# A message-passing layer on one core: clears held to four in flight, first stage in a new order, two results kept in PSUM

## The reference, cut to what matters

```
ssp(v) = softplus(v) - log 2
h   = x @ W_in2f
W   = (ssp(edge_attr_64 @ Wf1 + bf1) @ Wf2 + bf2) * edge_weight1
m   = segment_sum(h[dst] * W, src, 50000)
m   = ssp(m @ Wo1 + bo1) @ Wo2 + bo2
out = layernorm(x + (x + m))
```

## Time and profile before

| | us |
|---|---|
| median of 3 runs | 1865.61 (1861.05 to 1866.87) |
| profiled execution | 1858.28, its span 1856.5 |
| busy in the span: PE | 1697.3 |
| DVE | 1489.3 |
| ACT | 1492.9 |
| POOL | 1441.4 |
| first stage: last scatter ends | 1398.4 |
| second stage: first PE work | 1403.57 |

### The profile page before, as it was taken

The page is one execution under the profiler, slowest core; times in us unless marked ns, Lnnn a source line. Parts: engine busy times, 40 slices in busy tenths (PEclk is TensorE's granted clock), DMA queues, the critical chain, the costliest instruction groups (busy, mean ns, idle before and its releaser), DMA issues. The chain is left out here.

```text
span 1856.5 us, 36676 instructions
## 1 busy us (share of the span) xinstructions
PE 1697.3 (91%) x11376; PEld 1532.2 (83%) x11376; DVE 1489.3 (80%) x3750; ACT 1492.9 (80%) x2945; POOL 1441.4 (78%) x1385
## 2 busy tenths in 40 slices
PE   3499899999999999999999998889976999999995
PEld 2378788888888888888888887778866999999995
DVE  2477788787888888888888786777765999999996
ACT  2477788778888788888888786776756999999996
POOL 7422488888887888878888888888754999999997
PEclk9699999999999999999999998999998999999998
DMA  9799866656566665666665666665675999999994
GB/s 354 251 356 372 266 123 112 126 112 125 115 125 122 112 123 114 124 125 112 125 120 116 119 122 113 114 118 108 116 185 170 333 363 362 360 360 364 357 366 174
DMA packets 177341, 363.47 MB, mean 196 GB/s; under 512 B 25622, under 2 KB 76264, under 8 KB 177148
## 3 DMA queue, kind: packets, MB, share of 16 engines
q1 hardware_dynamic: 101128, 257.75, 39.8%
q0 software_dynamic: 75136, 102.45, 32.4%
q10 hardware_dynamic: 884, 0.92, 0.2%
HBM read 206.90 MB, written 154.12 MB: 194 GB/s over the span
## 5 line engine op out<-in xcount | busy, mean ns | idle before, releaser
L354 POOL DMA_INDIRECT acc<-sums,src_ix x392 | 637.2, 1626 | 141.6 <-issue 116.0
L341 POOL DMA_INDIRECT xg<-in_x,dst_t x392 | 401.4, 1024 | 215.6 <-issue 114.6
L780 DVE SCALAR_TENSOR_TENSOR m_l<-pair,wgt_t,m_h 128x256 fp32r<-128x256 f32 x392 | 171.6, 479 | 230.5 <-ACT m_h L621 206.6
L385 POOL TENSOR_SCALAR sums<-sums,neg_mean,rstd 128x256 f32<-128x256 f32 x392 | 283.2, 733 | 10.2
L495 PE MATMUL pair<-m_h,same 128*128 128x256 f32 (+1 forms) x980 | 244.8, 285 | 30.4 <-ACT sums L628 21.9
L621 ACT ACTIVATE m_h<-pair,wgt_t 128x256 fp32r<-128x256 f32 x392 | 165.0, 475 | 99.5 <-PE pair L409 57.6
L495 PE MATMUL pair<-m_l,same 128*128 128x256 f32 (+1 forms) x980 | 241.8, 281 | 0.0
L409 PE MATMUL pair<-wo_h,msg_h 128*128 128x256 f32 (+1 forms) x784 | 230.9, 295 | 6.0 <-DVE m_l L780 5.2
L495 PEld LDWEIGHTS pair<-m_h,same 128*128 128x128 f32 (+1 forms) x980 | 185.1, 189 | 52.2 <-issue 34.9
L576 ACT ACTIVATE zs<-pair,bf 128x512 f32<-128x512 f32 x196 | 124.1, 685 | 125.8 <-PE pair L433 99.5
L409 PE MATMUL pair<-wo_h,msg_l 128*128 128x256 f32 (+1 forms) x784 | 222.0, 283 | 0.0
(11 more groups left out here) (97 smaller groups left out, 5249.8 us busy)
## 6 DMA issues: line engine op xcount, KB each, us to landing
acc<-fill SPq DMA_DIRECT2D x197, 256.0 KB
xg<-in_x SPq DMA_DIRECT2D x97, 512.0 KB, 6.4
sums<-acc SPq DMA_DIRECT2D x97, 512.0 KB, 6.8
out<-sums SPq DMA_DIRECT2D x97, 512.0 KB, 4.7
attr<-in_edge_attr SPq DMA_DIRECT2D x196, 128.0 KB
srcb<-in_src_rows SPq DMA_DIRECT2D x98, 256.0 KB
xg<-in_x,dst_t POOLq DMA_INDIRECT x392
acc<-sums,src_ix POOLq DMA_INDIRECT x392
```

What stands on the lines that cost most here:

```text
L341: pool.indirect_dma_start(xg[0:g.p, g.xs, r], None, t["x"], bass.IndirectOffsetOnAxis(ap=dst_t[0:g.p, r, g.n:g.n + 1], axis=0)).then_inc(x ...
L354: pool.indirect_dma_start(acc, bass.IndirectOffsetOnAxis(ap=src_ix[g.slot][0:g.p, r:r + 1], axis=0), sums[0:g.p, g.slot, r], None, compute ...
L385: last = pool.tensor_scalar(normed[0:g.p, g.n % NRING, r], res[0:g.p, u, r], neg_mean[0:g.p, u, r:r + 1], rstd[0:g.p, u, r:r + 1], ALU.add ...
L780: dve.scalar_tensor_tensor(out=m_l[0:g.p, r], in0=bank[6][0:g.p, k * D:(k + 1) * D], scalar=col(wgt_t, r, g), in1=m_h[0:g.p, r].bitcast(F3 ...
```

## The change

- SP: every clear waits for the clear four before it (four semaphores); the wait for the first gather after 8 clears is gone; the last rows are part of the same loop, so there are 198 clears in it.
- Rings: `RING` 12 to 13, `XRING` 11 to 12, `AHEAD` 23 to 24.
- The softplus result is written over its PSUM banks 2 and 3, and the message over bank 5, in place of the SBUF tiles `ssp` and `msg`, which are gone. `ssp_high`, `ssp_low`, `msg_high`, `msg_low` read PSUM. So `filter1` now waits for `ssp_low`, and `w_of` for `msg_low`.
- The three orders are new. `summed(0)` has lag 2 (was 3) and stands last, `summed(1)` keeps lag 3; `keep_y` has lag 3 (was 4); `compare` is four stages; most ACT and DVE stages have a lag less.
- SP: x for the second stage is loaded a group a step in the last steps, not at once at the end.
- `biases` is a piece of `first_weights` that now comes before step 0. Tiles of the second stage lie elsewhere.

```diff
-RING = 12
-XRING = 11
+RING = 13
+XRING = 12
-AHEAD = 23
-EARLY_CLEARS = 8
+AHEAD = 24
+IN_FLIGHT = 4
...
             def clear_to(count):
                 nonlocal clears
                 for c in range(clears, min(count, CLEARS)):
-                    sp.dma_start(acc[c * CLEAR * P:(c + 1) * CLEAR * P, :].rearrange("(p k) d -> p (k d)", k=CLEAR), fill[:, 0:CLEAR].rearrange("p k d -> p (k d)")).then_inc(cleared, 16)
+                    a, b = c * CLEAR * P, min((c + 1) * CLEAR * P, N + R * P)
+                    wait(sp, cleared[c % IN_FLIGHT], c // IN_FLIGHT * 16)
+                    sp.dma_start(acc[a:b, :].rearrange("(p k) d -> p (k d)", k=CLEAR),
+                                 fill[0:(b - a) // CLEAR].rearrange("p k d -> p (k d)")).then_inc(cleared[c % IN_FLIGHT], 16)
                 clears = max(clears, min(count, CLEARS))
-            clear_to(EARLY_CLEARS)
-            sp.wait_ge(xg_in[0], 16 * R)
             clear_to(FIRST_CLEARS)
...
                 clear_to(FIRST_CLEARS + (n - 1) * CLEARS_A_STEP)
+                if G - XRING <= n - 2:
+                    fetch_x(group((n - 2) % XRING))
...
-                wait(pe, ssp_sb, g.n * H)
+                wait(pe, sspl_sb, g.n * H)
...
-                    wait(pe, msg_sb, g.n * H + m)
+                    wait(pe, msgl_sb, g.n * H + m)
...
-            run((w_of(1), 2), (summed(0), 3), (h_of(0), 1), (summed(1), 3), (filter1, 0), (turn_x(0), 0),
-                (out1(0), 2), (turn_x(1), 0), (w_of(0), 1), (h_of(1), 1), (out1(1), 2), before={1: filter_bias})
+            run((w_of(1), 2), (summed(1), 3), (turn_x(0), 0), (turn_x(1), 0), (out1(0), 2), (h_of(0), 1), (filter1, 0),
+                (w_of(0), 1), (out1(1), 2), (h_of(1), 1), (summed(0), 2), before={1: filter_bias})
...
-            run((keep_y(0), 4), (msg_high(1), 3), (ssp_high(0), 2), (ssp_high(1), 2), (keep_h(0), 2), (absolute(0), 1),
-                (absolute(1), 1), (expo(0), 1), (m_high(0), 3), (keep_y(1), 4), (expo(1), 1), (x_high(0), 1), (loga(0), 1),
-                (loga(1), 1), (x_high(1), 1), (keep_h(1), 2), (m_high(1), 3), (a_high, 0), (msg_high(0), 2), before={1: weights})
+            run((x_high(0), 1), (keep_y(0), 3), (x_high(1), 1), (ssp_high(0), 1), (msg_high(1), 2), (ssp_high(1), 1), (keep_y(1), 3),
+                (a_high, 0), (m_high(0), 2), (keep_h(0), 1), (absolute(0), 0), (absolute(1), 0), (expo(0), 0), (expo(1), 0),
+                (loga(0), 0), (loga(1), 0), (msg_high(0), 1), (m_high(1), 2), (keep_h(1), 1), before={1: weights})
...
-                    dve.scalar_tensor_tensor(out=msg[:, m], in0=bank[5][:], scalar=bias_w[:, m:m + 1], in1=h_sb[:, m],
+                    dve.scalar_tensor_tensor(out=bank[5][:], in0=bank[5][:], scalar=bias_w[:, m:m + 1], in1=h_sb[:, m],
...
-                    low(msg_l[:, m], msg[:, m].rearrange("f (r e) -> f r e", r=R), msg_h[:, m], msgl_sb)
+                    low(msg_l[:, m], bank[5][:].rearrange("f (r e) -> f r e", r=R), msg_h[:, m], msgl_sb)
...
-                    dve.scalar_tensor_tensor(out=ssp[:, h], in0=bank[2 + h][:], scalar=neg_bf1[:, h:h + 1], in1=zs[:, h],
+                    dve.scalar_tensor_tensor(out=bank[2 + h][:], in0=bank[2 + h][:], scalar=neg_bf1[:, h:h + 1], in1=zs[:, h],
...
-                    low(ssp_l[:, g.par, h], ssp[:, h].rearrange("m (r e) -> m r e", r=R), ssp_h[:, g.par, h], sspl_sb)
+                    low(ssp_l[:, g.par, h], bank[2 + h][:].rearrange("m (r e) -> m r e", r=R), ssp_h[:, g.par, h], sspl_sb)
...
-            run((m_low(0), 3), (message(0), 2), (x_low(0), 1), (softplus(0), 1), (softplus(1), 1), (x_low(1), 1),
-                (m_low(1), 3), (message(1), 2), (a_low, 0), (msg_low(0), 2), (target, 3), (msg_low(1), 2), (ssp_low(0), 1),
-                (ssp_low(1), 1), (compare, 2), before={1: first_weights, 2: tables, 3: second_weights})
+            run((x_low(0), 1), (message(1), 2), (x_low(1), 1), (msg_low(1), 2), (ssp_low(0), 1), (ssp_low(1), 1), (a_low, 0),
+                (compare(0), 2), (m_low(0), 2), (compare(1), 2), (compare(2), 2), (message(0), 1), (compare(3), 2), (softplus(0), 0),
+                (msg_low(0), 1), (softplus(1), 0), (m_low(1), 2), (target, 2),
+                before={0: biases, 1: first_weights, 2: tables, 3: second_weights})
```

More of the change, by code:

```diff
@@ L155, in build @@
         a_h, a_l = (sb(n, [P, R, P], F32R) for n in ("a_h", "a_l"))
-        zs, ssp = (sb(n, [P, H, 512]) for n in ("zs", "ssp"))
+        zs, h_sb = (sb(n, [P, H, 512]) for n in ("zs", "h_sb"))
         ssp_h, ssp_l = (sb(n, [P, 2, H, R, P], F32R) for n in ("ssp_h", "ssp_l"))
@@ L173, in build @@
         grown = [zs, h_sb]
-        ssp2, ssp2_h, ssp2_l = [ssp, msg], ssp_h, ssp_l
+        ssp2 = [sums[:, MRING + DEPTH + NRING + k].rearrange("p r d -> p (r d)").rearrange("p (h n) -> p h n", h=H) for k in range(2)]
+        ssp2_h, ssp2_l = ([b[:, k] for k in range(2)] for b in (ssp_h, ssp_l))
         wo2 = attr[:, G % ARING].rearrange("p (h d) -> p h d", h=H)
@@ L181, in build @@
         dst_in, src_in, wgt_in, tab_made = sem("dst_in"), sem("src_in"), sem("wgt_in"), sem("tab_made")
-        bo1_in, fill_made, cleared = sem("bo1_in"), sem("fill_made"), sem("cleared")
+        bo1_in, fill_made = sem("bo1_in"), sem("fill_made")
+        cleared = [sem(f"cleared{u}") for u in range(IN_FLIGHT)]
         made = sem("made")
@@ L224, in build @@
         block = ctx.enter_context(nc.Block())
-        CLEARS = N // P // CLEAR
+        CLEARS = -(-(N + R * P) // (P * CLEAR))
         TABLES = 1 + R
-        assert N // P % CLEAR == 0
-        CLEAR_REST = len(range(CLEARS * CLEAR * P, N + R * P, CLEAR * P))
+        assert (N + R * P) % CLEAR == 0
         def rows_of(ap, g):
@@ L293, in fetch_m @@
                 sp.dma_start(m_in[0:g.p, g.n % MRING].rearrange("p r d -> p (r d)"), rows_of(acc, g).rearrange("(p r) d -> p (r d)", r=R)).then_inc(m_got[g.n % MRING], 16)
[L295 to L299, removed]
             def store(g):
@@ L304, in store @@
                 sp.dma_start(rows_of(out, g).rearrange("(p r) d -> p (r d)", r=R), normed[0:g.p, u].rearrange("p r d -> p (r d)")).then_inc(stored[u], 16)
-            for n in range(G - XRING, G):
+            for n in range(G - 1, G):
                 fetch_x(group(n % XRING))
@@ L348, in stage @@
                         if g.n == 0:
-                            pool.wait_ge(cleared, 16 * (CLEARS + CLEAR_REST))
+                            for u in range(IN_FLIGHT):
+                                pool.wait_ge(cleared[u], 16 * len(range(u, CLEARS, IN_FLIGHT)))
                         pool.wait_ge(src_ready, g.n + 1)
@@ L526, in stage @@
                             for sp2, w in ((ssp2_h, wo2_h), (ssp2_h, wo2_l), (ssp2_l, wo2_h)):
-                                last = pe.matmul(o, sp2[:, g.par, h, r, 0:g.p], w[:, h, :], start=False, stop=h == H - 1 and sp2 is ssp2_l)
+                                last = pe.matmul(o, sp2[g.par][:, h, r, 0:g.p], w[:, h, :], start=False, stop=h == H - 1 and sp2 is ssp2_l)
                     last.then_inc(o_ps, 1)
@@ L736, in a_low, with compare, stage @@
                 low(a_l[:, :, 0:g.p], attr[:, g.n % ARING].rearrange("f (r e) -> f r e", r=R)[:, :, 0:g.p], a_h[:, :, 0:g.p], al_sb)
-            def compare(g):
-                dve.wait_ge(srcb_in[g.n % SRING], (g.n // SRING + 1) * 16)
-                wait(dve, y_ps, (g.n - 1) * 2)
-                sources = srcb[0:g.p, g.n % SRING].rearrange("x (r e) -> x r e", r=R)[:, :, 0:g.p]
-                for a in range(R):
+            def compare(a):
+                def stage(g):
+                    if a == 0:
+                        dve.wait_ge(srcb_in[g.n % SRING], (g.n // SRING + 1) * 16)
+                        wait(dve, y_ps, (g.n - 1) * 2)
+                    sources = srcb[0:g.p, g.n % SRING].rearrange("x (r e) -> x r e", r=R)[:, :, 0:g.p]
                     dve.scalar_tensor_tensor(out=same[0:g.p, g.par, FROM[a]:FROM[a] + R - a, 0:g.p], in0=sources[:, a:R],
@@ L746, in compare @@
                                              accum_out=alike[0:g.p, g.par, a:a + 1]).then_inc(same_ready, 1)
+                return stage
             def target(g):
@@ L818, in ssp2_low @@
                 wait(dve, o_ps, (g.n - 1) * 2)
-                low(ssp2_l[:, g.par].rearrange("m h r e -> m (h r e)"), ssp2[g.par][:].rearrange("m h n -> m (h n)"),
-                    ssp2_h[:, g.par].rearrange("m h r e -> m (h r e)"), ssp2l_sb)
+                low(ssp2_l[g.par].rearrange("m h r e -> m (h r e)"), ssp2[g.par][:].rearrange("m h n -> m (h n)"),
+                    ssp2_h[g.par].rearrange("m h r e -> m (h r e)"), ssp2l_sb)
             def residual(g):
```

24 lines of the change are left out of this document (12 added, 12 removed).

## The result

The changed kernel takes 1891.03 us (median of 4 runs, 1888.32 to 1892.29) against 1865.21 for the kernel before in the same comparison: ratio 1.014, 95% interval 1.0119 to 1.0161. Slower by 26 us, where 18 us faster was forecast; the range of 1820 to 1879 does not hold it. The profiled execution has a span of 1886.6 us against 1856.5: 30.1 us to explain.

What follows compares the result with a forecast made beforehand. It took POOL and PE to finish the first stage nearly together, after a head paced by SP's clears. Terms -17 + 0 - 7 + 6 gave -18 us: execution 1840, median 1848, range 1820 to 1879.

Steps and rivals of the forecast that it cites:

- The head: The stretch up to about 212 us: `filter1` of group 12 was to start at 202 against 218.8, 17 us earlier.
- A clear costs 0.97, 1.10 and 0.80 us with four in flight: Head, SP's clears: 0.97 us for the first 36, 1.10 for the next 16, 0.80 late.
- The third rival: Head: the hold starves the clears, 1.0 us each from the start, 30 us on the head, +12, 1878; chance 0.10.
- The hold cures the early stalls: Head: ACT's 13.3 us and DVE's 37.6 us stalls, read as instruction fetch queued behind clears, were to go.
- SP's list of clears sets the first scatter: Head: SP's list sets the pace and reaches group 12's load at 194, with the first scatter at 199.
- PE's step: Groups 12 to 97: 13.36 us a step against 13.35 before, so 0 over 85 steps.
- the ring: Longest dependency chain from one `filter1` to the next in the new order, through DVE and ACT: 13.06 us.
- The stalls took 0.33: ACT stalls that PE feels: 0.36 us a step in the old order, 0.30 forecast in the new.
- the 0 that was taken for them: DVE passes writing PSUM: no extra time per pass, within -0.05 to +0.15 us; two passes lie in the ring.
- POOL's cover: Scatters and gathers less disturbed by DVE: up to 30 us less on POOL, mostly cover, not time.
- The drain: From `filter1` of group 97 to the last scatter's end: 38 us against 45, 7 us less.
- the 6: Near the end: 6 us given back, as POOL, nearly tied with PE, delays x.

Runs made afterwards that it cites:

- e2: The kernel before with only the hold added (four clears in flight): 1888.52 us, ratio 1.014.
- e1: The changed kernel without the hold on clears: 1879.63 us, ratio 1.0071 against the kernel before.
- e6: The kernel before with no clears in the first step, then 20 a step: 1895.66 us in a single run.
- e5: The kernel before with POOL's first gathers paced by the groups turned, clears untouched: 1863.1 us, ratio 0.999.
- e4: The changed kernel with the old rings (`RING`, `XRING`, `AHEAD` 12, 11, 23): 1887.75 us, ratio 1.0117 against the kernel before.
- e16: The changed kernel, its own order, without the hold and with paced gathers: 1834.63 us, ratio 0.987 against the kernel before.
- e17: The changed kernel without the hold and with paced gathers, run again on another chip: 1870.07 us, ratio 1.0015 against the kernel before.
- e9: The kernel before with 68 clears first in place of 36: 1886.88 us, ratio 1.0134.
- e10: The changed kernel without the hold, with 84 clears first in place of 36: 1860.41 us, ratio 0.9999 against the kernel before.
- e3: The changed kernel with softplus and message back in SBUF tiles and the old rings: 1936.33 us, ratio 1.0375 against the kernel before.
- e7: The changed kernel with three other orders, whose longest ring is PE's own 12.6 us, hold kept: 1916.5 us, ratio 1.0276 against the kernel before.
- e8: The changed kernel with three other orders, without the hold and with paced gathers: 1883.08 us, ratio 1.0093 against the kernel before.
- e11: The kernel before with paced gathers and 24 clears a step in place of 16: 1897.28 us, ratio 1.0192.

## Why the prediction was wrong

**The head, -17, was +22.5, and this step alone turns the sign.** Three of its claims failed.
- *A clear costs 0.97, 1.10 and 0.80 us with four in flight.* It costs 1.22, 1.40 and 0.80 to 0.92. The value was chosen near an idle load of 196 KB; the other bound, 1.18 from the 512 KB stores under load, was the better guide, since these clears run beside gathers and loads too. e2 prices the hold at 23.5 us in the old order, e1 at 11 in the new one. The third rival had this mechanism, with 1.0 us a clear from the start, 30 us on the head and a time of 1878; its size was too small, and it got 0.10.
- *The hold cures the early stalls, since these are engines whose instruction fetch is queued behind clears.* The stalls grew from 37.6 to 54.9 us on DVE and from 13.3 to 35.7 on ACT. e6 took the early clears away and kept the stall; e5 paced the gathers and cut it to 11.9. `filter1` of group 2 tells which part of the change lengthens the stall: it starts at 77.2 us before and at 78.8 with the hold (e2), but at 89.8 with the new order and the old rings (e4) and at 93.1 with all of it (93.5 without the hold, e1). So the new order brings some 11 us and the rings 3; the hold brings nothing here, and its price comes in the steps after: from group 2 to 12 the changed kernel takes 148.2 us and e1 139.1. Why the new order stretches the stall stays open. That these are instruction fetches finds no support either. The trace marks some DMA packets as instruction, and between 32 and 78 us of the kernel before, while ACT and DVE stand, only the two other queues have any (packets, MB, share):

```profile
q1 hardware_dynamic: 5213, 9.41, 55.1%
q0 software_dynamic: 1585, 4.33, 28.7%
```

  In the changed kernel there is none between 32 and 95 us. And from 250 to 1050 us e16 has 80 such packets and e17 77, though only e17 has the stalls. The Trainium skill ("Runtime: NRT & Kernel Launch", Instruction fetch mechanics) calls crossing an instruction block "mostly hidden"; these traces show nothing against it. By that rule the stalls have another cause, as the prediction itself granted; which one, no run shows.
- *SP's list of clears sets the first scatter.* In the kernel before PE's turning of x set it, by way of the last gather [9.56 us ahead of 206.91]; the clears were just in time. In the changed kernel the clears are late by 16.0 us. Two conditions nearly tied: slowing one costs in full, and quickening one brings nothing. e9 and e10 had their clears out at about 184 and 187, and their first scatters came at 216 and 219.

The page "DMA: Bandwidth & Descriptors" of the Trainium skill would have made the hold free (an estimate of 0.65 us a clear with four in flight). The page gives its fit for DMAs that GpSimd issues, and these are SP's, beside other traffic. The trace has twice the estimate in the first 52 clears. The page's remark on late confirmations of writes to HBM would go with that, but no run separates it from the load on the engines.

**PE's step: the ring was right, the term was not.** The ring of 13.06 measures 13.20, and 13.26 in e3. DVE's passes into PSUM take 754 ns against 746 and 741 before: the 0 that was taken for them is 0.01. The stalls took 0.33 where 0.30 was forecast. So the step is 13.53 for a forecast 13.36, of which 0.14 is the ring and 0.03 the stalls, and the term, put at 0, is +15.8 us over 85 steps. It has two parts. Up to group 80 the step grows from 12.96 to 13.54, +39 us; from there on it falls from 14.91 to 13.53, -23 us, since PE hardly waits for x any more. The forecast's 0 was the balance of these two, and the old mean of 13.35 hid them. The term counts in the changed kernel, as POOL waits for it at the end.

**POOL's cover, up to 30: half.** Over the whole stage a scatter's mean fell from 1626 to 1606 ns and a gather's from 1024 to 1008: with 392 of each, 14 us. With the four gathers that moved ahead of the first scatter POOL was 0.22 us a group faster, 18 us at group 79, and spent nearly all of it from there on, waiting for PE's ring. The 49 us of e3 don't measure this term, since e3 was locked.

**The drain, -7 and +6: right in sign, both small.** From `filter1` of group 97 to the last scatter's end 35.9 us (forecast 38), and from 1192 us on PE waits only 3.9 us for x, so the 6 wasn't spent. The second stage begins as before, with 0.9 us more.

Sum by what was measured, at PE: +22.5 + 15.8 - 9.1 = +29.2; the rest of the span adds 0.9. The forecast had -17, 0, -1. The step that failed is thus the head first, and PE's term second. That the second failed doesn't show at POOL, whose chain came out 1.9 us from the old one only because its own gain and PE's longer step cancelled.

## What to carry to other kernels

Where a phase ends on two conditions, find both and how far apart they are before you price a change on one; the releaser of the last wait names only one of them. A limit on DMAs in flight is a throttle: price it by stores under the load they will run in, and look at the GB/s row for what it leaves idle. Compare a new step with the old one stretch by stretch, not with a mean that holds another wait. A faster engine may lose to phase: two loops of nearly the same period can meet in each step, and only a timeline of both shows that. So compare two kernels in several stretches before you put a difference down to the edit: a lock in one of them can be all of it. A gain that rests on the absence of stalls should be measured on a second chip before it is believed.

## What the runs showed that was not expected

- Two engines locked in step through DMA traffic: a load issued 0 to 1 us after the start of the last scatter of a group delays its landing by about 0.7 us (e9: 1.01 against 0.30 us of waiting, 54 steps), and the quicker engine stays in that place for 40 groups. Five of twenty profiles have this lock (e3, e7, e8, e9, e11).
- Paced gathers cut DVE's stall in the head from 37.6 to 11.9 us, with the clears unchanged; holding the clears left it at 33.3 and 15.8 us in two pieces (e2).
- The same program took 1834.6 us on one chip and 1870.1 on another, where the kernel before differed by 1.5 us (1865.1 and 1866.5).
- In such a lock a scatter can meet the same DVE passes each time: its mean was 1795 ns in e3 while locked and 1632 after, with the same tiles and the same order.
- More clears ahead of the first load cured no head: the load of attr queued behind them held ACT 46.3 us at a stretch (e9), longer than the stall of 37.6 us that DVE has in the kernel before.
